# The transposed rows of all three late token groups kept in DRAM by the second stage, and none transposed again at the end

## What is computed

```python
# mixer
h = layernorm(ln(x), ln_w, ln_b)
Q, K, V = split(h @ W_in + b_in, 3)          # rotary part on Q and K
A = sum(cos_sim(K) * V, axis=tokens)         # one row per batch
x = x + ln((A * Q) @ W_out + b_out + ln(x))
# experts: E = 8 of width 256, top 2 of 8, and a shared pair of width 512
n = ln(x)
gates = softmax over the top 2 of n @ gate_w
routed = sum_e gates_e * (gelu(n @ w1_e + b1_e) @ w2_e + b2_e)
shared = gelu(n @ shared_w1 + shared_b1) @ shared_w2 + shared_b2
out = x + ln(routed + shared)
```

## Time and profile before

| what | before |
|---|---|
| three runs, us | 937.12, 937.21, 938.23 |
| profiled execution, us | 936.45 |
| its span, first to last instruction, us | 934.6 |
| mean granted TensorE clock | 0.981 |
| TensorE busy | 878.2 us, 94% of the span |
| DVE busy | 637.1 us, 68% |
| ACT busy | 434.3 us, 46% |
| POOL busy | 397.2 us, 42% |
| moved by DMA | 212.17 MB, mean 227 GB/s |

### The profile page before, as it was taken

One profiled execution on the slowest core, in us unless ns is written; L12 is line 12 of the kernel. 1 busy time (PEld: TensorE's weight loads), 2 busy tenths in 40 slices (PEclk: granted clock), 3 DMA queues, 4 the chain that ended last, 5 costly groups with the idle time before them and its releaser, 6 DMA issues.

```text
span 934.6 us, 14747 instructions
## 1 busy us (share of the span) xinstructions
PE 878.2 (94%) x4542; PEld 724.3 (77%) x4542; DVE 637.1 (68%) x1366; ACT 434.3 (46%) x825; POOL 397.2 (42%) x321
## 2 busy tenths in 40 slices
PE   4999999999999989999999898599999999999986
PEld 3788787878888677777777777488888889888765
DVE  6967977977965756656566677366656666665777
ACT  5335345245253142241322445266666666666464
POOL 1457467367454000000000100376777668763175
PEclk9999999999999999999999998799999999999998
DMA  8328878878658886776443799497887888888999
GB/s 305 114 68 299 305 263 305 290 271 314 225 205 319 344 324 218 277 270 238 168 138 132 263 349 289 127 225 148 150 158 148 181 185 164 151 139 194 333 262 223
DMA packets 87962, 212.17 MB, mean 227 GB/s; under 512 B 11576, under 2 KB 20024, under 8 KB 82512
## 3 DMA queue, kind: packets, MB, share of 16 engines
q1 hardware_dynamic: 62928, 165.43, 49.0%
q0 software_dynamic: 19360, 43.60, 24.9%
q10 hardware_dynamic: 5600, 2.20, 1.1%
HBM read 118.09 MB, written 93.11 MB: 226 GB/s over the span
## 4 chain that ended last, share of the span: by engine, by line
PE 43%; issue 10%; DVE 9%; DMA 4%; ACT 4%; POOL 2%; DVEq 0%; POOLq 0%; ACTq 0%; SPq 0%
PE bank L1836 3%; PE bank L1834 3%; PE bank L1835 3%; PE bank L1821 3%; PE bank L1592 3%; PE bank L1851 3%; PE bank L1593 3%; PE bank L1594 3%; PE bank L1853 3%; PE bank L1852 3%; DMA f_scratch<-ro,dst 2%; PE bank L1843 2%; PE bank L1742 1%; PE bank L1587 1%; PE bank L1744 1%
## 5 line engine op out<-in xcount | busy, mean ns | idle before, releaser
L1541 POOL DMA_INDIRECT f_scratch<-ro,dst x71 | 112.5, 1584 | 53.3 <-SPq L594 25.2
L1533 POOL DMA_INDIRECT xr<-n_scratch,ids x71 | 70.1, 987 | 77.9 <-issue 54.8
L1592 PE MATMUL bank<-wkv_hi,h_hi 128*128 128x512 f32 x248 | 97.3, 392 | 0.0
L1594 PE MATMUL bank<-wkv_hi,h_lo 128*128 128x512 f32 x248 | 96.7, 390 | 0.0
L1593 PE MATMUL bank<-wkv_lo,h_hi 128*128 128x512 f32 x248 | 96.6, 390 | 0.0
L1336 DVE TENSOR_TENSOR ro<-bank,b2b 128x512 f32<-128x512 f32 x71 | 49.1, 692 | 67.8 <-PE bank L1853 56.1
L1834 PE MATMUL bank<-we,x_hi 128*128 x284 | 86.3, 304 | 0.2 <-DVE x_lo L1316 0.2
L1836 PE MATMUL bank<-we,x_lo 128*128 x284 | 80.5, 283 | 0.0
L1835 PE MATMUL bank<-we,x_hi 128*128 x284 | 80.4, 283 | 0.0
L655 ACT ACTIVATE sq<-kb 128x512 f32<-128x512 f32 x32 | 20.2, 633 | 127.8 <-DVE kb L963 127.8
L1510 POOL TENSOR_TENSOR zr<-zv,half 128x4 f32<-128x4 f32 x8 | 8.1, 1009 | 120.6 <-DVE zv L1096 120.6
(11 more groups left out here) (242 smaller groups left out, 2518.6 us busy)
## 6 DMA issues: line engine op xcount, KB each, us to landing
xg<-in_X SPq DMA_DIRECT2D x15, 1024.0 KB, 7.4
we<-expert_scratch SPq DMA_DIRECT2D x6, 2048.0 KB, 13.2
w_lo<-in_w SPq DMA_DIRECT2D x16, 512.0 KB, 5.4
expert_scratch<-w_hi SPq DMA_DIRECT2D x16, 512.0 KB, 2.8
expert_scratch<-w_lo SPq DMA_DIRECT2D x16, 512.0 KB, 4.1
q_scratch<-qh SPq DMA_DIRECT2D x8, 1024.0 KB, 3.9
q_scratch<-qb SPq DMA_DIRECT2D x8, 1024.0 KB, 6.2
q_hi<-q_scratch SPq DMA_DIRECT2D x8, 1024.0 KB, 4.9
```

Of the source, the lines that this page charges most:

```text
L1533: pool.indirect_dma_start(xr[u][:, :], None, n3_dram, bass.IndirectOffsetOnAxis(ids[:, i:i + 1], 0)).then_inc(row_in[u], 16)
L1541: pool.indirect_dma_start(f_dram, bass.IndirectOffsetOnAxis(dst[:, i:i + 1], 0), ro[i % NRO][:, :], None, compute_op=ALU.add).then_inc(r_s ...
L1592: pe.matmul(dst, hi(k), w_hi(k), start=(k == 0), stop=False)
L1594: last = pe.matmul(dst, lo(k), w_hi(k), start=False, stop=(k == KD - 1 and not more))
```

## The change

All three late groups now go the way of the first. At the steps s = 2, 4 and 6 SP stores both parts of groups 1, 3 and 5 to a `turned_scratch` three times as large, and ACT waits for each pair of stores a step later. For i = 1 SP loads `nc_hi` at place 64 of its loop and `nc_lo` at place 66. For i = 2 ACT's queue loads both after the last tile, behind `c2_raw`. The transposes, ACT's rounding and DVE's subtraction of groups 3 and 5 are gone from the end, with their PSUM banks `tc` and semaphores. Some tiles change places in SBUF, and SP's loads of `f` for the second and third late group and of x2 wait for the eight products of h of i = 0 and 1 (`sc_full`).

```diff
-    nt_dram = dram("turned_scratch", (2, P, KD * G))
+    nt_dram = dram("turned_scratch", (len(LATE), 2, P, KD * G))
@@
-                if s == LATE[0] + 1:
-                    sp.wait_ge(t2_free, 2 + t2_use(LATE[0], KD - 1) + 1)
+                if s - 1 in LATE:
+                    sp.wait_ge(t2_free, 2 + t2_use(s - 1, KD - 1) + 1)
                     for c, part in enumerate((n_hi, n_lo)):
-                        sp.dma_start(nt_dram[c], part[:, :, :].rearrange("p k t -> p (k t)").bitcast(F32)).then_inc(turned, 16)
+                        sp.dma_start(nt_dram[LATE.index(s - 1), c], part[:, :, :].rearrange("p k t -> p (k t)").bitcast(F32)).then_inc(turned, 16)
@@
-            def load_n3(i):
-                sp.dma_start(n3c[i][:, :, :], n3_groups[LATE[i]]).then_inc(n3c_in[i], 16)
+            def load_turned(i, c):
+                sp.dma_start((nc_hi, nc_lo)[c][i][:, :, :].rearrange("p k t -> p (k t)").bitcast(F32), nt_dram[i, c]).then_inc(n3c_in[i], 16)
@@
                 if i == NRT - E:
                     sp.wait_ge(oe_full, NRT - E)
-                    load_n3(1)
+                    load_turned(1, 0)
+                if i == NRT - E + 2:
+                    load_turned(1, 1)
@@
-            sp.wait_ge(tc_full, KD)
+            sp.wait_ge(sc_full, KS * 2)
             load_f(LATE[1])
-            sp.wait_ge(c_split, KS)
             load_f(LATE[2])
-            sp.wait_ge(tc_full, KD * (len(LATE) - 1))
@@
-                    if g == LATE[0] + 1 and k == 0:
-                        act.wait_ge(turned, 32)
+                    if g - 1 in LATE and k == 0:
+                        act.wait_ge(turned, 32 * (LATE.index(g - 1) + 1))
@@
             act.dma_start(c2_raw[:, :, :], sw2.rearrange("(k p) d -> p k d", p=P)).then_inc(c_in[1], 16)
-            act.dma_start(n3c[2][:, :, :], n3_groups[LATE[2]]).then_inc(n3c_in[2], 16)
-            for k in range(KD):
-                nc_hi_part(1, k)
+            for part, c in ((nc_hi, 0), (nc_lo, 1)):
+                act.dma_start(part[2][:, :, :].rearrange("p k t -> p (k t)").bitcast(F32), nt_dram[2, c]).then_inc(n3c_in[2], 16)
@@
-            nc_lo_parts(1)
@@
-                if (what, i, m) == ("h", 1, 1):
-                    nc_lo_parts(2)
@@
-                    late_turn(1)
@@
-                pe.wait_ge(tc_free, 4 + KD * i)
+                pe.wait_ge(n3c_in[i], 32)
@@
-                    if i == 1 and m == 1:
-                        late_turn(2)
```

More of the change, by code:

```diff
@@ L212, in sandwich_kernel @@
         ro = [at(f"ro{i}", 192.125 + 2 * i, [P, D]) for i in range(NRO)]
-        f = [at(f"f{g}", kb_, [P, GT, D]) for g, kb_ in enumerate((64, 104, 16, 24, 32, 40, 48, 56))]
-        n3c = [None, at("n3c1", 8 * LATE[1], [P, GT, D]), at("n3c2", 72, [P, GT, D])]
-        nc_hi, nc_lo = ([at(f"{n}{i}", kb_, [P, KD, G], F32R) for i, kb_ in enumerate(kbs)] for n, kbs in (("nc_hi", (128, 164, 80)), ("nc_lo", (0, 96, 88))))
+        f = [at(f"f{g}", kb_, [P, GT, D]) for g, kb_ in enumerate((64, 104, 40, 24, 32, 16, 48, 56))]
+        nc_hi, nc_lo = ([at(f"{n}{i}", kb_, [P, KD, G], F32R) for i, kb_ in enumerate(kbs)] for n, kbs in (("nc_hi", (128, 16, 80)), ("nc_lo", (0, 24, 88))))
         c1_hi, c1_lo = at("c1_hi", 136, [P, KD, SH], F32R), at("c1_lo", 8, [P, KD, SH], F32R)
@@ L227, in sandwich_kernel @@
         x2c = {g: at(f"x2c{g}", kb_, [P, GT, D]) for g, kb_ in zip(ADDED + LATE[-1:], (128, 136))}
-        c2_raw = at("c2_raw", 8 * LATE[-1], [P, KS, D])
+        c2_raw = at("c2_raw", 72, [P, KS, D])
         fst, fmv = at("fst", 192.125, [P, NT, 6]), at("fmv", 193, [P, NT, 2])
@@ L238, in sandwich_kernel @@
         rank_ps, ids_ps = bank[2], bank[0]
-        tc = ((bank[7], bank[2], bank[5], bank[6]), (bank[1], bank[0], bank[7], bank[2]))
         sc = (bank[0], bank[1], bank[3], bank[4])
@@ L587, in _ @@
             sp.wait_ge(xt_full, 2 * NX)
-            sp.wait_ge(turned, 32)
-            sp.dma_start(nc_hi[0][:, :, :].rearrange("p k t -> p (k t)").bitcast(F32), nt_dram[0]).then_inc(turned, 16)
+            sp.wait_ge(turned, 32 * len(LATE))
+            load_turned(0, 0)
             sp.dma_start(c1_hi[:, :, :].rearrange("p k h -> p (k h)").bitcast(F32), ws_dram[0, 0]).then_inc(turned, 16)
@@ L599, in _ @@
                     c = (i - NT) // 4 * 2
-                    sp.dma_start(nc_lo[0][:, c:c + 2, :].rearrange("p k t -> p (k t)").bitcast(F32), nt_dram[1, :, c * G:(c + 2) * G])\
+                    sp.dma_start(nc_lo[0][:, c:c + 2, :].rearrange("p k t -> p (k t)").bitcast(F32), nt_dram[0, 1, :, c * G:(c + 2) * G])\
                       .then_inc(c_in[0], 16)
@@ L842, in scale_row_before @@
                     scale_row(i - 2)
-            def nc_hi_part(i, k):
-                act.wait_ge(tc_full, KD * (i - 1) + k + 1)
-                act.activation(nc_hi[i][:, k, :], tc[i - 1][k][:, :], ACT.Copy).then_inc(nc_hi_done, 1)
             act.wait_ge(o_full, NO)
@@ L896, in _ @@
                     c2_hi_part(m)
-                if (what, i, m) == ("h", 1, 1):
-                    for k in range(KD):
-                        nc_hi_part(2, k)
                 for g, j in y_of[what, i, m]:
@@ L1336, in o_out @@
                 dve.tensor_tensor(ro[i % NRO][:, :], oe_ps[u][:, :], row, ALU.add).then_inc(oe_free, 1)
-            def nc_lo_part(i, k):
-                dve.wait_ge(nc_hi_done, KD * (i - 1) + k + 1)
-                dve.tensor_tensor(nc_lo[i][:, k, :], tc[i - 1][k][:, :], nc_hi[i][:, k, :].bitcast(F32), ALU.subtract)\
-                   .then_inc(tc_free, 1)
             dve.sem_inc(oe_free, 2)
             dve.sem_inc(th_free, 2)
-            dve.sem_inc(tc_free, 4)
             dve.sem_inc(fc_free, 2)
@@ L1362, in _ @@
             o_out(PRE, PRE % 2, e)
-            def nc_lo_parts(i):
-                for k in range(KD):
-                    nc_lo_part(i, k)
             def hc_lo_part(i, m):
@@ L1857, in expert @@
                 return pe.value_load(owner[0:1, i:i + 1], min_val=0, max_val=E - 1)
-            def late_turn_part(i, k):
-                pe.wait_ge(tc_free, KD * (i - 1) + k + 1)
-                transposes(tc[i - 1][k], n3c[i], k).then_inc(tc_full, 1)
             pe.wait_ge(owner_ready, 1)
@@ L1878, in _ @@
             h_turn(PRE, PRE % 2)
-            def late_turn(i):
-                pe.wait_ge(n3c_in[i], 16)
-                for k in range(KD):
-                    late_turn_part(i, k)
             def late_h_part(i, m, lo):
@@ L1898, in _ @@
             pe.wait_ge(xt_free, PRE + 1)
-            pe.wait_ge(turned, 64)
+            pe.wait_ge(turned, 32 * len(LATE) + 32)
             pe.wait_ge(c_in[0], 64)
```

3 lines of the change are left out of this document (1 added, 2 removed).

## The result

The changed kernel took 946.15 us (median), the kernel before beside it 937.32: a ratio of 1.0094, 95% interval 1.0065 to 1.0122, so +8.8 us (6.1 to 11.4). The forecast was 941.8 with a range of 937.8 to 943.8. The direction was right, the size was not. The profiled execution took 943.77 us, the fastest of the changed kernel's; its span is 941.9.

The account below looks back on a forecast made before the run. TensorE was taken as the bound mid-program and DVE's chain at the end. End -2.4 + 2.5 = +0.1, plus stall +3.5 and clock +1.5, gave +5.1 us: forecast 941.8 us, range 937.8 to 943.8.

Parts of the forecast that it names:

- From there on everything ... hangs on DVE's sequence, so I let it shift as a block: -2.4 us: At the end: removing the third late group's four nc_lo subtractions on DVE brings everything behind them 2.40 us earlier.
- Two signs: At the end: 60.7 us from DVE's first f tile to span end; TensorE's wait at group 0's o about 3 us.
- The last scatter, +2.5: At the end: larger loads on ACT's queue and nc_lo1 delay the last scatter-add's landing, and f, by 2.5 us.
- ACT has c2_hi between its gelus, and that waits for c2_raw as before: At the end, group 1's h: starts no earlier than the gelus free its banks; rest has cover, no cost counted.
- Rival (e): Worse: nc_lo1, issued early, delays scatter 67, which releases 68 to 70, and pieces add: 943.6 or more; chance 0.09.
- The end altogether: Expert stage's end: -2.4 from DVE's removed work and +2.5 from the late scatter, sum +0.1 us.
- The second stage: Step s = 4: turned stores ahead of fo stall TensorE, +3.5, and the clock falls, +1.5; nothing at s = 6.
- (b): Stall at s = 4 comes but the scatters aren't delayed: 937.6 or 939.1, by the median 0.7 more; chance 0.14.
- (c): Stall at s = 4 is hidden, DVE's wait under 2.45 us; only +0.1 left, 937 to 937.5; chance 0.08.
- (d): Faster: added transfers cost nothing, DVE's 2.40 us gain remains: 934.1, 934.8 by the median; chance 0.07.

Follow-up runs that it names:

- d: Changed kernel with the nc_hi2 and nc_lo2 loads moved off ACT's queue to SP, behind its first four f loads: +9.5 us (6.6 to 12.3) against before.
- i: Changed kernel with 0.25 MB of nc_hi2 loaded in place of the 2 MB of nc_hi2 and nc_lo2: +5.5 us (3.0 to 8.1) against before.
- l: Changed kernel with the edits of a and i together: -1.3 us (-3.4 to 0.7) against before.
- a: Changed kernel with the turned stores moved behind the first two fo stores of their step: +2.6 us (0.8 to 4.4) against before.
- f: Changed kernel with ACT's four c2_hi casts (and DVE's c2_lo) behind the first late group's gelus: +8.8 us (6.6 to 11.1) against before.
- m: l with the four c2_hi casts moved behind the gelus, as in f: -2.9 us (-5.0 to -0.9) against before.
- e: Changed kernel with the nc_lo1 load issued two places earlier, right behind nc_hi1: +9.8 us (7.2 to 12.4) against before.
- b: Kernel before, plus the second stage's turned stores of all three late groups, end as before: +4.1 us (2.3 to 5.9) against before.
- k: b with its turned stores of all three steps behind the first two fo stores: -2.3 us (-4.1 to -0.4) against before.
- h: Kernel before with DVE's four nc_lo subtractions of the third late group left out: -0.1 us (-1.7 to 1.5) against before.
- j: Kernel before with one 1 MB transfer more on ACT's queue, behind c2_raw and n3c2: +1.2 us (-0.6 to 3.0) against before.
- n: Kernel before with two late groups' turned rows kept, stored behind fo, and the third turned in the end: +0.2 us (-2.0 to 2.4) against before.
- o: Kernel before with the edits of p and h together: -2.2 us (-4.5 to 0.2) against before.
- p: Kernel before with 0.25 MB instead of 1 MB in each of the two x2c loads: -0.8 us (-3.2 to 1.7) against before.
- g: Kernel before with its own two turned stores at s = 2 behind the first two fo stores: -0.2 us (-2.3 to 2.0) against before.
- c: Changed kernel's end with one late group's turned stores only, loaded for all three groups: +3.9 us (2.0 to 5.8) against before.

## Why the prediction was wrong, and where it was right

**The step that failed: "From there on everything ... hangs on DVE's sequence, so I let it shift as a block: -2.4 us".** The chain of waits names what came last, not by how much. DVE's four subtractions were on it, and leaving them out alone gave -0.1 (-1.7 to 1.5), where -2.4 was counted. On DVE itself the sum was nearly right: its stretch from the first tile of `f` shrank by 2.0 us, and its last addition came 0.6 us later than before. What was wrong is that the span ends with DVE. The sum had no term for what the DMA queues have to move from the first `f` load on, and that ended the span: 5.7 us behind DVE's last addition instead of 2.6. With it fell the second half of the argument, that what delays `f` and what DVE saves can be summed: the one acts on both limits, the other on one. Two signs told it: from DVE's first tile of `f` to the end of the span there were 64.2 us, not 60.7 (before 63.1), and TensorE did not wait at `o` of group 0 at all, where about 3 us were expected.

**The last scatter, +2.5: right in size.** It landed 11.49 us after its issue, +2.1 to the first `f` load, and turns by packet were seen again. But the price of these loads is not that of the scatter alone: d put the scatter right and moved the 2 MB among the `f` loads, and no gain showed. What is paid is the 2 MB ahead of or among the `f` loads (i: -3.3 without 1.75 MB of them, and -3.9 in l against a). The way to DVE was another too: it stood only 0.85 us for `f`.

**"ACT has c2_hi between its gelus, and that waits for c2_raw as before": false, and without a price that could be measured here.** Before it did not wait; after it waits 4.38 us and TensorE 3.03. The transposes had covered it. Taking that wait away gave 0.0 with full loads (f), some 1.6 with light ones (m against l, with overlapping intervals). `nc_lo1`, issued at 854.83, was part of it, and its earlier issue gained nothing (e). Rival (e) named this transfer, though with another victim.

**The end altogether:** +0.1 forecast, +3.9 (2.0 to 5.8) measured. This is the error. Of the 3.8 between them, 2.4 are the gain that did not come. The other 1.4 can be the megabytes, which cost 3.3 (changed kernel less i) where I had 2.5, and the late `c2_raw`, as far as it shows; i is still 1.4 above b. Each of these is smaller than the uncertainty of a difference between two kernels, and how they divide stays open. In the two traces alone the end's +3.66 is a first `f` load that comes 2.56 us later and 1.10 us more from there to q0's last packet.

**The second stage:** +5.0 forecast, +4.1 (2.3 to 5.9) measured; moving the stores gave back 6.2, 6.4 and 6.8 us in three pairs (a, b with k, i with l). The mechanism was right in each link: landing 12.85 (some 12 forecast), DVE's wait 6.71 (5.5 to 6.4), two idle pieces of 1.99 and 2.23 (1.2 and 2.3), half clock for 3 us behind them, nothing at s = 6. The stall was undersized by 0.7: I added a megabyte's time to s = 2's stall, but DVE's wait grew by 6.71 - 3.35 = 3.4 for it.

**Rivals.** (b) and (c) were refuted by the same rows. (d) did not happen, but its 2.4 us were refuted by h for a reason that it did not name. (e) came nearest in time.

## What to carry to other kernels

Where the end of a program stores results while it still computes, read the DMA share in the windows behind the last compute instruction before pricing anything on the chain: if the queues are full there, time saved on an engine may bring nothing, as the 2.4 us of DVE here, and each megabyte moved into that stretch counts (here 1.2 us in j, where none is not excluded, 1.9 in i, 2.2 in l against a). In this kernel a 256 KB store landed 9.48 us after its issue with 4 MB ahead of it on its queue and 12.85 us with 5 MB, so a large transfer that nobody waits for belongs behind the small one whose landing frees a buffer; here that move was worth over 6 us. And when work is taken out, ask which transfer was in flight beneath it.

## What the runs showed that I had not expected

Behind the last stores the span takes time of its own, and not always the same. In m no engine and hardly a packet is at work after 936, and the span ends at 938.4, with SP waiting 2.2 us on TensorE's sequencer at L77; in the changed kernel that wait was 1.1, in the kernel before 0.2:

```profile
SPq L77 <- DMA out<-f: 1.7, 1, 1.7
SPq L77 <- PEq L77: 0.2, 1, 0.2
```

The long one appears where POOL's stores on q0 were still moving when SP's were (m, queues from 930 to 934):

```profile
q1 hardware_dynamic: 411, 0.75, 51.7%
q0 software_dynamic: 190, 0.33, 45.4%
```

Before, q0 had moved its last packets by 931.6; the queues from 931.6 to the end of the span have q1 alone:

```profile
q1 hardware_dynamic: 211, 0.36, 32.2%
```

Over all nineteen traces this is regular. In fourteen the span ends 3.07 to 3.10 us behind the last packet of q0, POOL's adding stores. In the other five (b, k, n, o, p) it ends 0.75 or 0.76 us behind the last packet of q1, the store of DVE's last addition, and 2.4 us behind that addition; there q0 had ended 3.2 to 4.2 us before the end. So the later of the two decides, and these are the limits that meet. In the kernel before they stood within 0.1 us of each other (931.56 + 3.07, 933.83 + 0.75); in the changed kernel q0 was later by 0.9 (938.86 + 3.07, 940.23 + 0.75), and lighter loads in p and o leave the end to DVE.

When q0 ends goes by the start and the load. From the first `f` load to its last packet it took 65.0 to 66.1 us with the end of the kernel before (before, b, g, h, k), 66.5 to 67.9 with the changed end (changed kernel, a, c, e, f), 63.6 and 64.3 in o and p, which move 17.36 MB from there on instead of 18.93, and 71.3 in d with 21.03. Why the changed end takes the longer of the first two is open, and so is what fills the 3.07 us behind q0.
